# Attention value products in pairs of units, and the copy of a finished group one unit sooner

## What is computed

```python
# 16 heads of 16 values; each query sees the 128 keys up to its own place, its own left out or last by the mask
dist = q_pos[:, :, None] - k_gpos[:, None, :]
allowed = (dist > 0) & (dist <= w) & (k_gpos[:, None, :] >= 0)
scores = jnp.where(allowed, jnp.einsum('bhnqd,bhnkd->bhnqk', qb, kb) * scale, NEG)
attn = softmax(scores); out = jnp.einsum('bhnqk,bhnkd->bhnqd', attn, vb)      # "local"
# beside it a small attention of every row to pooled rows ("latent"), projected: remote
gate = sigmoid(local @ gl_w + remote_h @ gr_w)
mixed = gate * local + (1.0 - gate) * remote_h
return mixed @ out_w + out_b
```

## Time and profile before

| | |
|---|---|
| median of 3 runs | 2029.63 us (2025.75 to 2030.84) |
| span of the profiled execution, first to last instruction | 1935.2 us |
| time of the profiled execution outside of its span | not given by the page; median less span is 94.4 us |
| TensorE busy | 1745.9 us, 90% |
| VectorE, ScalarE, GpSimd busy | 65%, 52%, 41% |
| value products (L1585) | 2048 records, from 104.7 to 909 us |
| granted TensorE clock, mean | 0.959 of full speed |

### The profile page before, as it was taken

The page is one execution under the profiler, slowest core; times in us unless marked ns, Lnnn a source line. Parts: engine busy times, 40 slices in busy tenths (PEclk is TensorE's granted clock), DMA queues, the critical chain, the costliest instruction groups (busy, mean ns, idle before and its releaser), DMA issues.

```text
span 1935.2 us, 41720 instructions
## 1 busy us (share of the span) xinstructions
PE 1745.9 (90%) x12978; PEld 1428.4 (74%) x12979; DVE 1265.4 (65%) x3121; ACT 997.8 (52%) x2314; POOL 792.4 (41%) x970
## 2 busy tenths in 40 slices
PE   0699999999999999988899995999999999999995
PEld 0466666666666666655788894999999999978884
DVE  3477788888888787876667766533333333367885
ACT  0366676767767666666433333444444444434553
POOL 2045555555555555555368774000000000067771
PEclk9889899999999888998799998999999999999997
DMA  2555556666555564562264533222222222247884
GB/s 46 87 83 84 100 90 109 111 111 107 104 105 104 101 107 90 95 115 91 67 204 162 172 129 127 63 73 73 73 73 71 72 73 73 76 153 184 223 203 75
DMA packets 175902, 205.94 MB, mean 106 GB/s; under 512 B 28209, under 2 KB 142450, under 8 KB 175762
## 3 DMA queue, kind: packets, MB, share of 16 engines
q1 hardware_dynamic: 153874, 161.66, 37.9%
q0 software_dynamic: 20736, 41.96, 8.3%
q10 hardware_dynamic: 1152, 0.52, 0.2%
HBM read 84.34 MB, written 68.81 MB: 79 GB/s over the span
## 4 chain that ended last, share of the span: by engine, by line
PE 70%; DVE 8%; ACT 6%; issue 5%; POOL 5%; DMA 2%; SPq 2%; ACTq 1%; POOLq 0%; DVEq 0%
PE bank L2295 5%; PE bank L1530 5%; PE bank L485 5%; PE bank L2296 4%; PE bank L487 4%; PE bank L2297 4%; PE bank L486 4%; PE bank L1585 4%; PE bank L1550 4%; PE bank L1532 3%; PE bank L1531 3%; ACT prob L1026 3%; PE bank L2316 3%; PE bank L2318 3%; PE bank L2317 3%
## 5 line engine op out<-in xcount | busy, mean ns | idle before, releaser
L2438 POOL DMA_INDIRECT f_y<-yg_scratch,index_all x128 | 129.8, 1014 | 552.8 <-DMA yg_scratch<-b_y 514.1
L897 POOL TENSOR_SCALAR_AFFINE_SELECT prob<-prob 128x512 f32<-128x512 f32 x256 | 163.4, 638 | 397.4 <-ACT prob L1026 397.3
L1026 ACT ACTIVATE prob<-bank 128x512 f32<-128x512 f32 (+1 forms) x512 | 249.1, 539 | 117.2 <-PE bank L1572 114.6
L2186 DVE TENSOR_TENSOR b_h<-b_h,bank 128x352 f32<-128x352 f32 x136 | 70.9, 521 | 291.7 <-ACT b_h L2134 291.7
L1305 DVE COPY_PREDICATED bank<-from_prev,bank 128x512 f32<-128x512 int32 x192 | 133.0, 693 | 107.5 <-PE bank L1550 103.7
L1308 DVE TENSOR_REDUCE row_max<-bank 128x4 f32<-128x512 f32 x256 | 177.3, 693 | 27.7 <-PE bank L1550 20.4
L2295 PE MATMUL bank<-wgu_h,bxT_h 128*128 x544 | 180.5, 332 | 0.7 <-DVE bxT_l L2181 0.3
L2296 PE MATMUL bank<-wgu_l,bxT_h 128*128 x544 | 176.9, 325 | 0.0
L2297 PE MATMUL bank<-wgu_h,bxT_l 128*128 x544 | 176.1, 324 | 0.0
L2134 ACT ACTIVATE b_h<-bank 128x352 f32<-128x352 f32 x136 | 63.2, 465 | 211.4 <-PE bank L2297 211.3
L1585 PE MATMUL bank<-prob,v_sb 128*32 128x256 f32 (+1 forms) x2048 | 164.1, 377 | 0.5 <-ACT pvT L1033 0.5
(11 more groups left out here) (338 smaller groups left out, 5104.0 us busy)
## 6 DMA issues: line engine op xcount, KB each, us to landing
bx<-xg_scratch SPq DMA_DIRECT2D x136, 128.0 KB, 2.1
yg_scratch<-b_y SPq DMA_DIRECT2D x136, 128.0 KB, 1.7
kS<-qk_h SPq DMA_DIRECT2D x128, 128.0 KB, 3.7
qS<-qk_h SPq DMA_DIRECT2D x128, 128.0 KB, 5.9
x_in<-in_L_attn_x_dram SPq DMA_DIRECT2D x16, 512.0 KB, 4.9
kS<-qk_l SPq DMA_DIRECT2D x64, 128.0 KB, 4.9
qS<-qk_l SPq DMA_DIRECT2D x64, 128.0 KB, 6.7
x_res<-in_L_attn_x_dram SPq DMA_DIRECT2D x16, 512.0 KB, 3.9
```

Of the source, the lines that this page charges most:

```text
L897: op = e.affine_select(out=own, in_=own, compare_op=ALU.is_gt, fill=0.0, base=0, pattern=[[0, HG], [1, P]], channel_multiplier=-1)
L1026: e.activation(prob[:, u % SLOTS, 2 * hp:2 * hp + 2, 0:w], src[:, :, 0:w], ACT.Exp, scale=SCALE).then_inc(keyed.frees[hp], 1)
```

## The change

On TensorE the value products of two units stand one behind the other at the end of each odd slot: units `u - 3` and `u - 2`. Even slots have none. On ScalarE the copy of a finished group stands one slot sooner and behind the exponentials of that slot, not ahead of them. Nothing is added or removed: 256 units, 64 copies.

```diff
@@ ScalarE, body
                         if u == 0 and live(before):
                             keep_att(before, 1)
-                        if u == 3 and live(prev):
-                            keep_pv(prev, G - 1)
-                        if u in (7, 11, 15) and live(i):
-                            keep_pv(i, (u - 7) // T)
                         if u == 4 and live(prev):
                             keep_local(prev, 0)
                             keep_remote(prev, 0)
                         if live(i):
                             exps(i, u)
+                        if u == 2 and live(prev):
+                            keep_pv(prev, G - 1)
+                        if u in (6, 10, 14) and live(i):
+                            keep_pv(i, (u - 6) // T)
@@ TensorE
-                def weigh(i, prev, buf, u):
-
-                    if u >= LAG:
-                        if live(i):
-                            weigh_values(i, buf, u - LAG)
-                    elif live(prev):
-                        weigh_values(prev, 1 - buf, UNITS + u - LAG)
+                def weigh_pair(i, prev, buf, u):
+
+                    for n in (u - LAG, u - LAG + 1):
+                        if n >= 0:
+                            if live(i):
+                                weigh_values(i, buf, n)
+                        elif live(prev):
+                            weigh_values(prev, 1 - buf, UNITS + n)
@@ TensorE, body
                         if live(i):
                             keyed_scores(i, buf, u)
-                        if u % T != LAG:
-                            weigh(i, prev, buf, u)
@@ TensorE, end of the slot
-                        if u % T == LAG:
-                            weigh(i, prev, buf, u)
+                        if u % 2 == 1:
+                            weigh_pair(i, prev, buf, u)
```

## The result

The changed kernel takes 2055.11 us (median of 4 runs, 2052.34 to 2057.76), the kernel before on the same chip 2030.24. The ratio is 1.0119, 95% interval 1.0094 to 1.0144: 24 us slower, where 8 were forecast.

What follows compares the result with a forecast made beforehand. A chain of waits through TensorE, ScalarE and GpSimd, not TensorE alone, was taken to bound the attention. 2029.6 + 4.5 (new waits) + 4 (clock) = 2038 us; its own case's range 2036 to 2046, with 2 in 10 outside 2018 to 2058.

Steps and rivals of the forecast that it cites:

- The unit price: TensorE value products: the second unit of a pair takes 0.44 us instead of 0.57, saving 0.13 us a pair.
- The 17 us that all pairs would give: Attention stage: 0.13 us saved over 128 pairs, about 17 us if no engine waited for anything else.
- Where it goes in a period: Shifts followed slot by slot through one 50.70 us attention period: +0.3 us each, +4.5 us over 15 periods.
- the copy ahead of `loc`: ScalarE, slot 6: `pvT` holds the next instruction 0.48 us, putting `loc` and TensorE's latent queries at +0.4 us.
- the first steps: Slots 13 to 5: shifts from the pairs and a slot 1 wait, ending at -0.2 us at slot 5's keyed scores.
- The new wait for the latent scores in slot 1: TensorE's query projection waits 0.4 us for VectorE to read the latent scores, starting 3.6 us behind the window.
- the pairs of slots 9 to 13: TensorE time saved in slots 9 to 12 is lost in waits, since ScalarE and GpSimd lead slots 9 to 13.
- The clock: Attention stage: stretches at granted clock 0.50, five before the change, priced at 4 us each; one more expected, +4 us.
- one such fall more: One added drop to granted clock 0.50 in the attention, +4 us; bounds -4 and +20 us.
- rival D: Clock falls in many more attention periods; five more with the waits give +24.5 us, 2054 us; chance 0.18.
- the wait before the first transposition: TensorE idle before the first transposition of the mixed rows, waiting for GpSimd: 1.06 us before, forecast 1.5 us.
- The fixed 94.4 us: Gap between the profiled execution's 1935.2 us span and the 2029.63 us median, taken as fixed time outside the span.

Runs made afterwards that it cites:

- after_again: The changed kernel run once more, unaltered, on another chip against the kernel before: 2054.09 us against 2032.0, ratio 1.0110.
- pairs_filler: Changed kernel plus unread TensorE products, four ahead of the first transposition of the mixed rows and two ahead of the second: 2009.72 us against 2019.25 before, ratio 0.9961.
- filler_first_only: Changed kernel with the copy at its old place, plus four unread products ahead of the first transposition only: 2019.27 us against 2032.0 before, ratio 0.9941.
- pairs_inner: Kernel before with pairs only at the ends of slots 9, 11 and 13, other units single, copy at its old place: 2042.82 us against 2033.28, ratio 1.0053.
- pairs_old_copy: Changed kernel with all pairs but the finished group's copy back at its old place: 2037.45 us against 2019.25 before, ratio 1.0126.

## Why the prediction was right in direction and a third of the size

**The unit price.** Right. 0.13 us a pair was forecast; a pair measured 1.00 against 2 x 0.57, which is 0.14. The reading of the one place in the old trace where value products followed products of the same form held to 0.01 us. The 17 us that all pairs would give did not come: at full clock a period of eight pairs is 0.2 us shorter, not 1.0.

**Where it goes in a period.** Right to a tenth. Forecast +0.3 us, measured +0.2 with the clock held. Its parts: the copy ahead of `loc`, forecast 0.48 on ScalarE, cost 0.49 a period alone and 0.40 with the pairs. The pairs gained 0.20, where the first steps had them at -0.2 by slot 5. The new wait for the latent scores in slot 1 came at 0.29 instead of 0.4; the projection started 3.55 us behind its window, forecast 3.6. That the pairs of slots 9 to 13 would be lost in the waits for GpSimd was right for the full clock; these waits grew from 1.3 to 2.4 us, forecast 2.3.

**The clock.** This is the step that failed, in size: "I expect one such fall more: +4 us". All 13 periods had one, nine or ten more. One cost less than the 4 us assumed, and it lasted 3.4 or 6.8 us and not 10.2. The price comes from kernels that differ in the unread products alone: the changed kernel took 689.36 us with 13 falls (690.46 in after_again), pairs_filler 663.26 with none, so the falls cost 26.1 to 27.2 us, 2.0 to 2.1 each. In the kernel before, three cost 667.71 - 660.30 = 7.4 us. 26.1 - 7.4, and 3.0 for the new waits, is 21.7 us in 13 periods, the difference of the two traces. The sum must close, being built of these same windows; that the loss is the clock's rests on the runs in which the added products took the falls away and the time went with them.

The mechanism was named, as rival D with a chance of 0.18, and its place was right, the wait before the first transposition, shown by filler_first_only and pairs_inner. That D's 2054 us lies beside the 2055 measured is in part luck: it has five more falls at 4 us, where nine or ten at about 2 came. What the forecast had no measure of was how steeply the falls grow: with 1.06 us of idle time there, three or four periods of 13 had one. With 1.62 us, unit 9 gone from in front of it, ten to 13 of 13 had (pairs_old_copy 10, pairs_inner 11, the changed kernel 13 twice).

The Trainium skill (TensorE: Matmul & The Clock Gate, A second HAM failure mode: psum-queue depth-cycling) had said that frequent short idles make the clock swing. The runs agree (waits of 1.62 and 0.80 us, 13 falls in 13 periods), and by it alone the forecast would have leaned further to the slow side. The other rule of the Trainium skill weighed there (TensorEngine Tiling (Array Packing), Key Properties), the drain at a change of mode, agrees with the 0.14 us of a pair, for which it has no figure; the gain of 17 us that the prediction drew from it did not come.

**The fixed 94.4 us.** Wrong, without a consequence for the difference: it wasn't time outside the span but a first profile with a shorter last stage (the second profile's execution took 1.8 us more than its span). Two numbers that lie 5% apart for one kernel ought to have been explained before being used.

**Left open.** Why the same 1.62 us wait goes with a fall in every period of one kernel and in ten or eleven of 13 of others. Whether the outer pairs add falls of their own to those of the inner ones. Why the last stage ran in 233 us once and in some 306 later: no run was made for it. The traces show where: in the two of 306 us ScalarE's L523 waits 11 times, 93 us together, for something that the profile calls `remote`, which is no instruction of this trace, and in the one of 233 us it never does.

## What to carry to other kernels

Before work is moved out of a wait, ask what it did there: beside taking time, it kept TensorE's clock. Moving 0.57 us from in front of a 1.06 us wait for GpSimd saved nothing at that place and cost about 2 us each time that the clock fell. Where TensorE has to wait for another engine in a loop, a few products that nothing reads, placed exactly in that wait, can be worth more than a reordering (here 0.4% for the old kernel, 0.8% with the pairs). At the one place tried where TensorE didn't wait they removed no fall and only cost.

A copy on ScalarE is cheap until it stands in front of the one for which TensorE waits. Look at whom the next instruction on that engine releases.

## What the runs showed of the hardware

The granted clock in the attention's periods took only two values, 1.00 and 0.50 (2.4 and 1.2 GHz). In the changed kernel it fell once a period, where only four transpositions of 128x128, a mask, a window and the keyed scores lay between two waits of 1.62 and 0.80 us, and not when four products of 128x512 (1.20 us from start to end) filled the first of these.

A period of the changed kernel is some 53.3 us with the fall of 6.8 us and 52.4 with that of 3.4, against 50.9 for pairs_filler: 2.4 and 1.5 us lost. Half of the stretch, 3.4 and 1.7 us, is what a kernel held by TensorE's clock alone would lose (an estimate from the clock's 0.50). So most of it was lost, though other engines lead part of the period. Over the 13 periods it is 26.1 us of 34; for the three falls of the kernel before, 7.4 of 12.

The falls fell into step with the kernel's loop: one long and one short in turn over the first eleven of 13 periods, in two profiles alike (689.4 and 690.5 us). The kernel before had three in one profile and four in another.
